# Layer-norm statistics taken in the phase before, and weight splits on ScalarE and VectorE beside the features, in a four-layer vision tower

## What is computed

```
h = conv(x) + position, with the class token in place 0
h += attention0(norm(h));  h += mixture of 32 experts(norm(h))      # layer 0
h += attention1(norm(h));  h += top-1 of 8 experts(norm(h))         # layer 1
h += attention2(norm(h))                                            # layer 2
y  = norm(h); y += attention(norm'(y)); y += mlp(y)
y += top-2 of 4 experts(norm'(y));  h += y
h += attention3(fake_quantised(norm(h)))                            # layer 3
y  = norm(h); y += attention(norm'(y)) with a mixing of tokens; y += mlp(norm'(y)); h += y
norm(x) = (x - mean(x)) / sqrt(var(x) + 1e-5), over the 192 features;  norm' also scales and shifts
```

## Time and profile before

| | us |
|---|---|
| median of 3 runs | 3163.15 (3162.18 to 3164.58) |
| the profiled execution's own time | 3168.47 |
| its span, first to last instruction | 3166.7 |
| PE, matmuls busy / weight loads busy | 2925.4 / 2680.8 |
| DVE, ACT, POOL busy | 2119.1, 1079.1, 642.8 |
| mean granted TensorE clock | 0.952 |

### The profile page before, as it was taken

The page is one execution under the profiler, slowest core; times in us unless marked ns, Lnnn a source line. Parts: engine busy times, 40 slices in busy tenths (PEclk is TensorE's granted clock), DMA queues, the critical chain, the costliest instruction groups (busy, mean ns, idle before and its releaser), DMA issues. The chain is left out here.

```text
span 3166.7 us, 56709 instructions
## 1 busy us (share of the span) xinstructions
PE 2925.4 (92%) x19995; PEld 2680.8 (85%) x19995; DVE 2119.1 (67%) x5308; ACT 1079.1 (34%) x2175; POOL 642.8 (20%) x767
## 2 busy tenths in 40 slices
PE   8989999999999999999998998897979989777887
PEld 7779999999999999999987887675868879766767
DVE  3857777767776777777777775234467567777866
ACT  2433233323333333333333333113435333333432
POOL 1311212221122212121202100112123111123431
PEclk9989999999999999999998999899989889979988
DMA  3011001000001000000010000560000000000000
GB/s 133 9 45 36 31 23 35 35 35 18 35 35 35 18 35 35 35 18 35 18 38 1 2 2 6 172 194 29 1 11 19 19 35 18 11 1 16 23 18 17
DMA packets 24033, 105.59 MB, mean 33 GB/s; under 512 B 4407, under 2 KB 9415, under 8 KB 18526
## 3 DMA queue, kind: packets, MB, share of 16 engines
q1 hardware_dynamic: 22222, 99.62, 9.1%
q0 software_dynamic: 1584, 3.30, 0.3%
HBM read 98.32 MB, written 6.64 MB: 33 GB/s over the span
## 5 line engine op out<-in xcount | busy, mean ns | idle before, releaser
L850 ACT ACTIVATE hid<-bank,dat 128x384 f32<-128x384 f32 (+1 forms) x912 | 555.6, 610 | 1144.5 <-PE bank L565 1028.4
L817 PE MATMUL bank<-w,hid_hi 128*128 128x384 f32 x2964 | 859.8, 361 | 2.2 <-DVE y_tok L864 1.6
L819 PE MATMUL bank<-w,hid_lo 128*128 128x192 f32 x2964 | 746.0, 252 | 0.0
L819 PEld LDWEIGHTS bank<-w,hid_lo 128*128 128x128 f32 x2964 | 571.6, 193 | 1.7
L817 PEld LDWEIGHTS bank<-w,hid_hi 128*128 128x128 f32 x2964 | 562.1, 190 | 5.5 <-issue 3.9
L882 DVE TENSOR_TENSOR hid_lo<-hid,hid_hi 128x384 fp32r<-128x384 f32 (+1 forms) x912 | 539.8, 592 | 31.6
L879 DVE CAST hid_hi<-hid 128x384 fp32r<-128x384 f32 (+1 forms) x912 | 340.8, 374 | 131.2 <-ACT hid L850 130.0
L893 DVE SCALAR_TENSOR_TENSOR h_tok<-bank,gate,h_tok 128x192 f32<-128x192 f32 x416 | 173.3, 417 | 249.5 <-PE bank L819 245.0
L565 PE MATMUL bank<-xa_hi,w_hi 128*128 128x384 f32 (+1 forms) x912 | 324.6, 356 | 12.7 <-DVEq L2229 12.4
L565 PE MATMUL bank<-xa_lo,w_hi 128*128 128x384 f32 (+1 forms) x912 | 323.0, 354 | 0.0
L565 PE MATMUL bank<-xb,w_lo 128*128 128x384 f32 (+1 forms) x912 | 322.3, 353 | 0.0
(11 more groups left out here) (361 smaller groups left out, 4569.1 us busy)
## 6 DMA issues: line engine op xcount, KB each, us to landing
raw<-in_L_exp SPq DMA_DIRECT2D x36, 1344.0 KB, 6.0
...
raw<-in_L_mlp SPq DMA_DIRECT2D x2, 1344.0 KB, 5.9
...
```

The source lines that it names most:

```text
L817: nc.tensor.matmul(o[:, 0:2 * D], hid_hi[k % 2][:, m, c], w2[j][:, m, :], start=m == 0, stop=False)
L819: ins = nc.tensor.matmul(o[:, 0:D], hid_lo[k % 2][:, m, c], w2[j][:, m, 0:D], start=False, stop=m == HC - 1)
L850: nc.scalar.activation(hid[(6 * k + m) % 3][:, 0:128 * nt], bank[4 + (6 * k + m) % 4][:, 0:128 * nt], func, bias=bias).then_inc(s["h_act"] ...
```

## The change

- **Statistics ahead.** `statistics` and `mean_of` take `bn_stats` and `bn_aggr` of a tile in the phase that writes it: the convolution, the end of each attention, the last expert's gathering, the routed experts' last step. Counters (`claim`, `made`) number them for the whole program. Features and norm phases start with one root over all 13 tiles and one pair of scales.
- **Division of the normalising.** Without `ln`, DVE now normalises blocks 1 and 2 and ACT 0 and 3; with `ln` it stays 2 for DVE.
- **Weights.** For attention 2 (`parts=True`) ACT copies the weights to the high part in two pieces and POOL subtracts; for the second attentions of layers 2 and 3 (`cleared=True` too) DVE subtracts, behind the features' low parts, and POOL clears only `q_t`. With `spread=True` (four experts, last mlp) ACT copies the first expert's weights beside the features, and DVE subtracts at the start of the experts phase (`low`). PE's first `up` waits for three of the four split steps.
- **Gates.** ACT and POOL split the gate weights in the features phase (`gate=`).
- **Clearings.** `n_tok` is cleared in the features phase, in five pieces (`clear=True`, `blocks_clear`), behind the weights; ACT waits for it only before its first blocks. `rel_a` is no longer cleared (except for attention 1), and `xs`, `p_t`, `v_x` no longer for the two second attentions.
- **Additions.** `h += y` is done tile by tile in the last expert's gathering (`onto=`); both add phases go. The output leaves in four DMAs, each waiting for its tiles.
- **Order.** DVE's `inner` (the outer norm of a second attention, 13 instructions) comes after the first `spread` and not first. DVE's loop over experts ends one pair earlier, with the last pair written out.

```diff
+            dve.wait_ge(ready, count)
+            nc.vector.bn_stats(stats[:, t, :], x[:, t, :]).then_inc(tile["stats"], 1)
+        def mean_of(dve, t, before):
+            dve.wait_ge(tile["stats"], before + t + 1)
+            nc.vector.bn_aggr(mv[:, t, :], stats[:, t, :]).then_inc(tile["mean"], 1)
+        def claim(name):
+            made[name] += TILES
+            return made[name] - TILES
...
-                def root(i):
-                    t0, n = TBLK[i]
-                    act.wait_ge(s["dve_step"].sem, b["dve_step"] + 2 * (t0 + n))
+                def root():
+                    act.wait_ge(tile["mean"], means)
                     nested = keep is not None
-                    nc.scalar.activation(rstd[:, 1, t0:t0 + n], mv[:, t0:t0 + n, 1], ACT.Sqrt,
+                    nc.scalar.activation(rstd[:, 1, :], mv[:, :, 1], ACT.Sqrt,
                                          bias=eps[:, 1:2] if nested else eps[:, 0:1],
                                          scale=1.0 + LN_EPS if nested else 1.0).then_inc(s["root"].sem, 1)
...
-                    piece(0)
-                    root(0)
-                    root(1)
-                    normalise(0)
-                    piece(1)
-                    root(2)
-                    normalise(1)
-                    root(3)
+                    if gate:
+                        nc.scalar.activation(gw[:, :, 0:g_n], gate_raw, ACT.Identity).then_inc(gate_w, 1)
+                    root()
+                    normalise(on_act[0])
                     if keep is not None:
                         nc.scalar.activation(once[:, 1, :], mv[:, :, 1], ACT.Sqrt, bias=eps[:, 0:1])\
                             .then_inc(s["root"].sem, 1)
+                    piece(0)
+                    for i in on_act[1:]:
+                        normalise(i)
+                    piece(1)
                     high(0)
                     piece(2)
-                    normalise(3)
                     piece(3)
                 else:
                     high(0)
@@ -482,43 +511,24 @@
                     high(i)
...
+                def scales():
+                    dve.wait_ge(s["root"].sem, b["root"] + 1)
+                    nc.vector.reciprocal(rstd[:, 2, :], rstd[:, 1, :]).then_inc(s["t_used"].sem, 1)
+                    dve.wait_ge(s["t_used"].sem, b["t_used"] + 1)
+                    nc.vector.scalar_tensor_tensor(rstd[:, 3, :], mv[:, :, 0], -1.0, rstd[:, 2, :], ALU.mult, ALU.mult)\
                         .then_inc(s["scale_full"].sem, 1)
...
-                    statistics(0)
-                    statistics(1)
-                    scales(0)
-                    statistics(2)
-                    scales(1)
-                    statistics(3)
-                    scales(2)
-                    scales(3)
-                    normalise(2)
+                    scales()
+                    for i in on_dve:
+                        normalise(i)
...
+                if gate:
+                    pool.wait_ge(gate_w, gate_at + 1)
+                    nc.gpsimd.tensor_tensor(gw[:, :, g_n:2 * g_n], gate_raw, gw[:, :, 0:g_n].bitcast(F32),
+                                            ALU.subtract).then_inc(gate_w, 1)
                 if norm_of is not None:
-                    pool.wait_ge(s["t_used"].sem, b["t_used"] + 5)
+                    pool.wait_ge(s["t_used"].sem, b["t_used"] + 1 + len(on_dve))
...
+            def blocks_clear(pool):
+                pool.wait_ge(s["t_full"].sem, b["t_full"] + 4)
+                for t0 in range(0, TILES, 3):
+                    ins = nc.gpsimd.memset(n_tok[:, t0:min(t0 + 3, TILES), :], 0.0)
+                ins.then_inc(s["bd_zero"].sem, 1)
+            phases.append(beside(dict(tensor=tensor, scalar=scalar, vector=vector, gpsimd=gpsimd), *others,
+                                 *([dict(gpsimd=blocks_clear)] if clear else [])))
...
+            def high(act, part):
+                act.wait_ge(s["w_in0"].sem, b["w_in0"] + 16)
+                o, x = (w1_hi[0][:, :, :], r1) if part == 0 else (w2[0][:, :, 0:D], r2)
+                nc.scalar.activation(o, x, ACT.Identity).then_inc(s["w_split"].sem, 1)
+            def low(dve):
+                dve.wait_ge(s["w_split"].sem, b["w_split"] + 2)
+                nc.vector.tensor_tensor(w1_lo[0][:, :, :], r1, w1_hi[0][:, :, :].bitcast(F32), ALU.subtract)\
+                    .then_inc(s["w_split"].sem, 1)
+                nc.vector.tensor_tensor(w2[0][:, :, D:2 * D], r2, w2[0][:, :, 0:D].bitcast(F32), ALU.subtract)\
+                    .then_inc(s["w_split"].sem, 1)
+            if spread:
+                return dict(sync=sync), dict(high=[lambda act: high(act, 0), lambda act: high(act, 1)]), dict(b, low=low)
...
+                def total(t):
+                    done = s["y_used"].sem, b["y_used"] + TILES * E + t + 1
+                    if onto is not None:
+                        dve.wait_ge(*done)
+                        nc.vector.tensor_tensor(onto[:, t, :], onto[:, t, :], res[:, t, :], ALU.add)\
+                            .then_inc(tile["updated"], 1)
+                        done = tile["updated"], updated + t + 1
+                    if stats_of is not None:
+                        statistics(dve, stats_of, t, *done)
...
                         g = 1.0 if E == 1 else gate[:, t, bass.ds(e, 1)]
                         nc.vector.scalar_tensor_tensor(res[:, t, :], o[:, 0:D], g, res[:, t, :], ALU.mult,
                                                        ALU.add).then_inc(s["dve_step"].sem, 1)
+                        if last and t:
+                            total(t - 1)
                         done_splits = 6 * min(k + 2, 4)
                         dve.wait_ge(s["dve_step"].sem, b["dve_step"] + STEPS * e + done_splits + t + 1)
                         nc.vector.scalar_tensor_tensor(res[:, t, :], o[:, D:2 * D], g, res[:, t, :], ALU.mult,
                                                        ALU.add).then_inc(s["y_used"].sem, 1)
+                        if last and t and stats_of is not None:
+                            mean_of(dve, t - 1, before)
+                    if last and t == TILES - 1:
+                        total(t)
+                        if stats_of is not None:
+                            mean_of(dve, t, before)
...
+                                                       ALU.mult, ALU.add).then_inc(tile["updated"], 1)
+                    for t in range(t0, t0 + nt):
+                        statistics(dve, res, t, tile["updated"], updated + t + 1)
+                    for t in range(t0, t0 + nt):
+                        mean_of(dve, t, means_before)
...
-                for m in pads[:-2] + pads[-1:]:
+                for m in () if cleared else pads[:-2]:
                     nc.gpsimd.memset(m.bitcast(F32) if m.dtype == F32R else m, 0.0)
-                if alone:
-                    weights_in(pool)
-                    nc.gpsimd.tensor_copy(wp_hi[:, 0:cols], wp_raw[:, 0:cols]).then_inc(s["att_hi"].sem, 1)
-                pool.wait_ge(s["att_hi"].sem, b["att_hi"] + (2 if low_rank else 1))
-                nc.gpsimd.tensor_tensor(wp_lo[:, 0:cols], wp_raw[:, 0:cols], wp_hi[:, 0:cols].bitcast(F32),
-                                        ALU.subtract).then_inc(s["pool_step"].sem, 1)
+                if not cleared:
+                    pool.wait_ge(s["att_hi"].sem, b["att_hi"] + (2 if parts else 1))
+                    nc.gpsimd.tensor_tensor(wp_lo[:, 0:cols], wp_raw[:, 0:cols], wp_hi[:, 0:cols].bitcast(F32),
+                                            ALU.subtract).then_inc(s["pool_step"].sem, 1)
                 pool.wait_ge(s["pool_step"].sem, b["pool_step"] + 1)
                 nc.gpsimd.memset(pads[-2], 0.0).then_inc(s["att_ready"].sem, 1)
-            if low_rank:
-                return dict(sync=sync, high=[lambda act: high(act, 0), lambda act: high(act, 1)], gpsimd=gpsimd)
+            def low(dve):
+                dve.wait_ge(s["att_hi"].sem, b["att_hi"] + 2)
+                nc.vector.tensor_tensor(wp_lo[:, 0:cols], wp_raw[:, 0:cols], wp_hi[:, 0:cols].bitcast(F32),
+                                        ALU.subtract).then_inc(s["pool_step"].sem, 1)
+            if parts:
+                return dict(sync=sync, high=[lambda act: high(act, 0), lambda act: high(act, 1)], gpsimd=gpsimd,
+                            low=[low] if cleared else [])
...
                 def blocks(t, g):
+                    if t == 0:
+                        act.wait_ge(s["bd_zero"].sem, b["bd_zero"] + 1)
...
+                def all_statistics(tiles):
+                    for y in tiles:
+                        statistics(dve, res, y, s["t_used"].sem, b["t_used"] + y + 1)
+                    for y in tiles:
+                        mean_of(dve, y, before)
                 def add_back(i, g):
                     for y in added_back(i, g):
                         dve.wait_ge(s["t_full"].sem, b["t_full"] + y + 1)
```

(12 more changed lines are left out.)

171 lines of the change are left out of this document (87 added, 84 removed).

## The result

The changed kernel takes 3124.57 us (median of 4, 3120.50 to 3126.66) against 3163.86 for the kernel before in the same comparison. The ratio is 0.9882, 95% interval 0.9866 to 0.9897: faster, by 39.3 us in this comparison, and by 34.5 when both were measured again (first experiment). The forecast was 35.

The account below looks back on a forecast made before the run. The prediction took a chain of waits at the seams between phases as the bound, neither DMA bandwidth nor PE's rate. Seam terms of 31.2 us and 4 for the clock gave 35: from 3163.15 to 3128 us, range 3110 to 3149.

Parts of the forecast that it names:

- these phases end 0.6 + 0.9 = 1.45 us later: Attentions ahead of seams 2, 6, 10, 11: statistics of the last tiles, taken at the tail, lengthen each by 1.45 us.
- DVE ends 3.35 us later: Routed phase ahead of seam 5: statistics don't fit between additions, so it ends 3.35 us later; seam gain only 0.9.
- 1.45 + 3.8 + four blocks: Seam 2: PE's queue binds; tail, ten matmuls, transposes (4.2) and eight matmuls (3.05) start logits at 186.15, gaining 4.1 us.
- the clock's term: PE's clock behind seams: 2 us at seam 2's logits, 1.5 each at seams 1 and 5; gain 4, bounds -9 to 14.
- Seam 9: Addition and 13 statistics go, 2.1 us return in the last expert; norm phase 5.9 not 9.5 us: 4.3, with clearing 5.1.
- With POOL idle this goes: Seams 6, 8, 10, 11: moving weights off POOL ends the stretching of DVE's low parts, 5.4, 7.5, 6.5 and 7.5 us.
- 27 us of stretch: Lengthening of DVE's low parts beside POOL's subtraction at seams 6, 8, 10, 11: 5.4, 7.5, 6.5, 7.5 us.
- the load wait and the series: Moved weights' price: loads land 4.2 to 6.1 us into seams 6, 8, 10; ACT's copy (1.47) and DVE's subtraction (2.76) add work.
- the copy stands in ACT's queue ahead of blocks 1 and 3: Seams 6, 8, 10: ACT's weight copy waits for loads landing 4.2, 6.1, 5.5 us in; seven tiles of normalising wait behind.
- a rival 2.45: Rival on dearer tails and ScalarE: ten tails 1 us dearer, four late loads 1.5 us each; gain 19, 3144 us; chance 0.17.
- the slower rival: TensorE falls to 1.2 GHz behind seams 1, 2, 3, 4, 8 after idle tails: 46 us lost against 35, 3174; chance 0.04.
- Marks: Trace signs for right, such as one root per features phase, seam 2's logits within 0.3 us, last DMA under 3.3 us.

Follow-up runs that it names:

- first experiment: The changed kernel executed a second time, unaltered, to see how far its trace repeats: 3126.11 us, ratio 0.9895 against the kernel before.

## Why the prediction was right, and where not

**Total.** 35 us forecast, 39.3 and 34.5 measured; 3128 against 3124.57. The sum of the seams ahead of their first products is 28.1 forecast and 28.4 measured, without seam 7. That it agrees so well is luck in part: seam 2 fell short by 1.8 and seam 9 did better by as much, and at seams 6, 8, 10 and 11 the numbers came true while the reason did not (below).

**Statistics.** The mechanism holds, and they are the largest part (10.8 us undone). The step that was too dear is "these phases end 0.6 + 0.9 = 1.45 us later": from PE's last product to the next phase's start it is 0.75 (seam 2; 1.05 in the second execution) and 1.04 (6, 10, 11) more. At seam 5 "DVE ends 3.35 us later" is right (3.1), and it eats more than the gain: the seam is 1.3 us shorter with the statistics back.

**Seam 2** failed in a term: "1.45 + 3.8 + four blocks". The ten matmuls took 6.25 and 5.55 us and not 3.86, because part of them ran at 1.2 GHz; in four other traces they took 6.8 us. I had priced a lost clock only behind the seam, in the clock's term, and not in the length of the very matmuls that hold it. The cheap tail made up for part.

**Seam 9** is 1.8 us better than forecast. The norm phase shrank as I said (5.8 us and not 9.5). The tail brought 1.4 and not 0.7, and 1.0 came in the quantise and features phases, which I had taken as unchanged; no run isolates that.

**Weights.** The forecasts for seams 6, 8, 10 and 11 (1.3, 2.6, 0.2, 3.7) came out at 1.4, 2.6, 0.3, 3.3, but not because of the move. "With POOL idle this goes" is right (no cast over 0.43 us), yet the run with the weights back on GpSimd gives the four seams together 1.0 us less, not 7.8 more. My working set the contention removed (27 us of stretch) against the load wait and the series, as the kernel before stands, and didn't ask what contention would be left were POOL early: 4.1, 7.5, 4.5 and 2.3 us. Nor did it ask what the statistics alone would bring: most of seam 11's gain is theirs (2.8 of 3.3). The wait that I found stood behind "the copy stands in ACT's queue ahead of blocks 1 and 3", and with the copies it was the change's largest flaw: 9.8 us once moved.

**Clock.** 4 us were too few for the pair of profiled executions. Behind first products 11.8 us were won (15.0 in the second execution), of which the clearing explains 2 to 3. PE's first 100 products behind seams 2 and 8, where no clearing is, take 3.3 and 1.3 us less; but the next 250 behind seam 8 take 1.7 more, and in two of the runs above, whose edits don't touch seam 2, the 3.3 there are 0.6. How much of the rest belongs to the change stays open, since attention 1 alone varies by 6 us between executions.

**Rivals.** None decided. The tails cost 0.75 to 1.05 us where I had 1.45 and a rival 2.45. No seam's clock fell for good; the slower rival's mechanism shows in the ten matmuls of seams 2, 6, 10 and 11 (6.25, 6.77, 6.91, 6.75 us against 3.86, 5.55, 5.55, 5.49), 6 us in all and mostly under ACT's work.

**Marks.** One root per phase; a first normalised tile 1.3 us after the phase's start (seam 8); transposes right behind the ten at seams 1 to 4; no DVE cast of features over 0.43 us at seams 6, 8, 10 and 11; logits 0.23 us behind; ACT's waits 2.33, 1.82, 3.71, 2.97 us at seams 5, 6, 8, 10; the last DMA 3.1 us: all as named, but for 1.82 where I said 2.

Undone one by one, the parts come to some 22 us by the traces: statistics 15.8, the addition 2.7 (6.2 at seam 9 less the 3.5 of statistics there, counted already), clearing 2.2, the output 1.8, gates 0.5, weights -1.0. By the median the statistics are 10.8, and the sum is some 17. The addition at the end was not undone. What is missing to 35 to 39 may be what two parts each suffice for, as at seam 2, and the clock. Only at seam 9 were two parts undone at once, so this isn't shown to the end.
